# The last eleven expert tiles' results added to their tokens by TensorE through weighted one-hots, 48 tiles scattered as before

## The reference, cut to what matters

```python
x = x + 0.5 * ffn(layernorm(x))
x = x + attn(layernorm(x))        # silu gates, a causal filter, projections
x = x + 0.5 * ffn(layernorm(x))   # the same weights
# ffn: E = 12 experts, K = 3 per token, D = 128, H = 512
gate_logits = x @ Wg
topw, sel = top_k(gate_logits, K);  topw = softmax(topw)
h = gelu(x @ Wup[e] + bup[e]);      y = h @ Wdown[e] + bdown[e]
out[token] = sum over its 3 experts of topw * y
```

## Time and profile before

| | us |
|---|---|
| median of 3 runs | 648.72 |
| lowest, highest | 647.03, 653.67 |
| the profiled execution, its own time | 651.71 |
| its span, first to last instruction | 650.0 |

### The profile page before, as it was taken

The page is one execution under the profiler, slowest core; times in us unless marked ns, Lnnn a source line. Parts: engine busy times, 40 slices in busy tenths (PEclk is TensorE's granted clock), DMA queues, the critical chain, the costliest instruction groups (busy, mean ns, idle before and its releaser), DMA issues.

```text
span 650.0 us, 18112 instructions
## 1 busy us (share of the span) xinstructions
PE 567.4 (87%) x4607; PEld 530.7 (82%) x4607; DVE 350.8 (54%) x1644; ACT 415.1 (64%) x1265; POOL 418.6 (64%) x432
## 2 busy tenths in 40 slices
PE   4569999998988999999989799999988989999514
PEld 4448999998987888889989698878988989999501
DVE  7882365462115688887417578888541613232216
ACT  2235676685666789777658588886755846666223
POOL 1137777777767773077776777017777777777773
PEclk9768999999999999999989899999999989999857
DMA  9745767789796775365678777536569788776145
GB/s 236 220 142 140 211 201 195 214 202 265 201 271 201 231 198 177 98 186 155 221 205 245 220 239 203 155 101 183 179 182 262 193 253 262 221 216 196 46 163 184
DMA packets 121797, 127.89 MB, mean 197 GB/s; under 512 B 17129, under 2 KB 84512, under 8 KB 121700
## 3 DMA queue, kind: packets, MB, share of 16 engines
q1 hardware_dynamic: 107508, 100.05, 52.7%
q0 software_dynamic: 12992, 26.11, 14.4%
q10 hardware_dynamic: 1200, 0.59, 0.3%
HBM read 96.62 MB, written 30.79 MB: 196 GB/s over the span
## 4 chain that ended last, share of the span: by engine, by line
PE 42%; issue 16%; POOL 16%; DVE 11%; DMA 8%; SPq 4%; ACT 2%; POOLq 1%; ACTq 0%; DVEq 0%
PE ps L808 16%; PE ps L819 16%; POOL xs L619 7%; POOL YG L632 5%; POOL xl L606 2%; PE ps L690 2%; PE ps L778 2%; DMA YG<-ys,SY 2%; DMA ys<-Ys 2%; DVE X L1071 2%; SPq L474 1%; DMA xs<-XN,SX 1%; DVE YG L1425 1%; DMA WU<-in_L_ffn_Wup_dram 1%; SPq L490 1%
## 5 line engine op out<-in xcount | busy, mean ns | idle before, releaser
L969 ACT ACTIVATE hT<-ps,BU 128x128 f32<-128x128 f32 x944 | 269.6, 370 | 116.2 <-PE ps L808 114.1
L808 PE MATMUL ps<-xT,WU 128*128 128x128 f32 x1888 | 255.9, 279 | 13.4 <-DMA WU<-in_L_ffn_Wup_dram 8.5
L819 PE MATMUL ps<-WD,hT 128*128 x1888 | 253.1, 278 | 9.0 <-DVE Ys L1486 8.1
L808 PEld LDWEIGHTS ps<-xT,WU 128*128 128x128 f32 x1888 | 234.5, 194 | 24.2 <-issue 14.6
L819 PEld LDWEIGHTS ps<-WD,hT 128*128 128x128 f32 x1888 | 232.9, 194 | 10.2 <-issue 10.1
L619 POOL DMA_INDIRECT xs<-XN,SX x144 | 145.2, 1008 | 97.7 <-ACT XN L891 54.3
L1486 DVE TENSOR_TENSOR Ys<-ps,BD 128x128 f32<-128x128 f32 x236 | 67.7, 289 | 218.0 <-PE ps L819 213.8
L632 POOL DMA_INDIRECT YG<-ys,SY x144 | 149.6, 1039 | 52.1 <-issue 41.3
L606 POOL DMA_INDIRECT xl<-xn,SG x59 | 60.1, 1019 | 30.5 <-issue 17.1
L641 POOL DMA_INDIRECT yk<-Ys,row x59 | 59.0, 1000 | 18.0 <-issue 16.5
L946 ACT ACTIVATE xT<-ps 128x512 f32<-128x512 f32 (+1 forms) x56 | 33.3, 595 | 5.4 <-PE ps L778 2.0
(11 more groups left out here) (246 smaller groups left out, 526.3 us busy)
## 6 DMA issues: line engine op xcount, KB each, us to landing
WU<-in_L_ffn_Wup_dram SPq DMA_DIRECT2D x236, 256.0 KB
ys<-Ys SPq DMA_DIRECT2D x42, 256.0 KB, 2.4
xl<-xs SPq DMA_DIRECT2D x118, 66.0 KB, 2.4
xl<-xs SPq DMA_DIRECT2D x59, 64.0 KB, 1.9
WD<-in_L_ffn_Wdown_dram SPq DMA_DIRECT2D x12, 256.0 KB, 5.3
WD<-yk SPq DMA_DIRECT2D x4, 768.0 KB, 7.2
xs<-XN,SX POOLq DMA_INDIRECT x144
YG<-ys,SY POOLq DMA_INDIRECT x144, 3.2
```

What stands on the lines that cost most here:

```text
L808: x = e.matmul(HB[i % 2][:, c * P:(c + 1) * P], WU[i % NW][:, c * P:(c + 1) * P], xT[m % 2][:, j * P:(j + 1) * P], start=True, stop=True)
L819: x = e.matmul(YB[i % 2][:, 0:D], hT[i % 3][:, c * P:(c + 1) * P], WDf[:, bass.ds(r + c * P, P)], start=(c == 0), stop=(c == C - 1))
L969: x = e.activation(hT[i % 3][:, c * P:(c + 1) * P], HB[i % 2][:, c * P:(c + 1) * P], ACT.Gelu, bias=BU[:, bass.ds(b + c, 1)])
```

## The change

Phase 3 scatters only its first 4 x GO = 48 tiles. The results of the last NO = 11 tiles (48 to 58) never go to memory: for each, VectorE builds in `hots(x)` four tiles 128 x 512 (one for each quarter) that hold a row's weight where the column is that row's token, and TensorE multiplies them with `Ys` in `spread(x)`: 4 quarters x 4 blocks = 16 products 128x128x128 in float32, accumulated in `psum[4]` to `psum[7]`. To have the weight, the three top logits travel with the row (`DX[1]` = 135), ScalarE takes their exponential (step "OA", slots 45, 49, 51) and VectorE forms the weight (`weigh`, step "OV", slots 46, 50, 52). `hots(x)` stands in VectorE's slot 50 + x of the phase and `spread(x)` in TensorE's slot 51 + x, both at most 58. `last(q)` adds `psum[4 + q]` at its end and for that waits until all eleven spreads are done (`s_hd`); the identity products of quarters 0 and 2 add on top of the bank. Since `yk` gets no rows from eleven tiles, it is filled with zeros first: twelve stores of 256 KB by SyncE in slots 12 to 34 of phase 0. `YL`'s quarters 0 and 1 now lie over `XN` and are loaded before the last `down`; 2 and 3 stay over `WD`. `FETCHED` and `FINAL_AT` change, `xT` has three buffers.

```diff
-DX = (D, D + 4)
+DX = (D, D + 7)
...
-FETCHED = tuple(min(K * NT, 6 + (13 * k) // 25) for k in range(NTL))
-FINAL_AT = tuple(next((k + 8 for k in range(NTL - 8) if FETCHED[k] >= K * (t + 1)), NTL) for t in range(NT))
+GO = NG - 3
+NO = NTL - 4 * GO
+FETCHED = tuple(min(K * NT, 6 + (3 * k) // 5) for k in range(4 * GO))
+FINAL_AT = tuple(next((k + 12 + k // 15 for k in range(42) if FETCHED[k] >= K * (t + 1)), NTL) for t in range(NT))
+HOTS = [("A", "OA", 45, 0), ("V", "OV", 46, 0), ("A", "OA", 49, 1), ("V", "OV", 50, 1), ("A", "OA", 51, 2),
+        ("V", "OV", 52, 2)]
+HOTS += [("V", "H", min(4 * GO + x + 2, NTL - 1), x) for x in range(NO)]
+HOTS += [("P", "H", min(4 * GO + x + 3, NTL - 1), x) for x in range(NO)]
...
-        xT = [sb(f"xT{i}", [P, 512]) for i in range(2)]
+        xT = [sb(f"xT{i}", [P, 512]) for i in range(3)]
...
+        YL = [XN[h][:, :, :].rearrange("p t d -> p (t d)")[:, 0:4 * K * D].rearrange("p (t k d) -> p t k d", k=K, d=D)
+              for h in range(NH)] + [YLW[:, 0:4], YLW[:, 4:8]]
+        HOT = [sT, tg, ag]
...
+            def zero_yk(x):
+                if x == 0:
+                    e.wait_ge(s_iota, 2)
+                e.dma_start(yk.rearrange("(p t k) d -> p t k d", t=NT, k=K)[:, 4 * (x // K):4 * (x // K) + 4, x % K, :],
+                            ag[NQ - 1][:].rearrange("p (t d) -> p t d", d=D)).then_inc(s_zk, 16)
...
+                if n == 0 and k % 2 == 0 and 12 <= k < 12 + 2 * NQ * K:
+                    zero_yk((k - 12) // 2)
...
-            e.wait_ge(s_dn, NI)
-            for m in range(4 * NG - NYS, 4 * NG):
+            for m in range(3 * NG + GO - NYS, 3 * NG + GO):
                 e.wait_ge(*stored(m))
             for q in range(NQ):
+                if q == 2:
+                    e.wait_ge(s_dn, NI)
...
-            for x in range(NTL):
+            e.wait_ge(s_zk, 16 * NQ * K)
+            for x in range(4 * GO):
                 while got < FETCHED[x]:
                     gather_y(2, got // K, got % K)
                     got += 1
...
+            def spread(x):
+                i = NI - NO + x
+                m, j = 3 * NG + TILES[i][2] // 4, TILES[i][2] % 4
+                if x == 0:
+                    for b in range(NQ):
+                        e.wait_ge(*drained(LAST[b]))
+                e.wait_ge(s_ho, x + 1)
+                e.wait_ge(s_Y, i + 1)
+                for q in range(NQ):
+                    for t in range(4):
+                        z = e.matmul(psum[4 + q][:, t * P:(t + 1) * P], HOT[x % 3][q][:, t * P:(t + 1) * P],
+                                     Ys[m % NYS][:, j, :], start=(x == 0 and t == 0), stop=True, skip_group_check=True)
+                z.then_inc(s_hd, 1)
...
+                if kind == "OA":
+                    w = size(GO + q)
+                    e.wait_ge(s_ol, q + 1)
+                    e.activation(dl[:, 4 * q:4 * q + w, :], dl[:, 4 * q:4 * q + w, :], ACT.Exp).then_inc(s_oe, 1)
+                    e.activation(go[:, q:q + 1], one[:, 0:1], ACT.Gelu)
...
+            def weigh(x):
+                a, b = 4 * x, 4 * x + size(GO + x)
+                e.wait_ge(s_oe, x + 1)
+                dv.on(e.tensor_scalar(em[:, a:b, :], dl[:, a:b, 1:K], 1.0, None, ALU.subtract))
...
+            def hots(x):
+                if x >= 3:
+                    e.wait_ge(s_hd, x - 2)
+                e.wait_ge(s_dv, dv.n)
+                for q in range(NQ):
+                    i = e.tensor_scalar(HOT[x % 3][q][:], io5[:], tb[:, x, q:q + 1], wr[:, x:x + 1], ALU.is_equal, ALU.mult)
+                i.then_inc(s_ho, 1)
...
             def last(q):
...
+                e.wait_ge(s_hd, NO)
+                e.wait_ge(s_dv, dv.n)
+                x4 = X[:, 4 * g:4 * g + 4, :].rearrange("p t d -> p (t d)")
+                e.tensor_tensor(x4, x4, psum[4 + q][:], ALU.add).then_inc(s_fin, 1)
```

More of the change, by code:

```diff
@@ L138, in schedule @@
             put("V", NTL * 3 + FINAL_AT[t], f"F{t % 4}", 0, t // 4, 1)
+    for engines, kind, at, x in HOTS:
+        put(engines, NTL * 3 + at, kind, 1, x, 2)
     return slots
@@ L162, in next_group @@
         return NG * n
+    if n == 3 and k >= 4 * GO:
+        return {4 * GO: NG * n + NG - 2, 4 * GO + 2: NG * n + NG - 1}.get(k)
     if k and k % 4 == 0 and k // 4 + 1 < NG:
@@ L201, in ring @@
         for step in SLOTS["P"][i]:
-            take(step, RING[step[0]])
+            if step[0] != "H":
+                take(step, RING[step[0]])
     return used, last
@@ L255, in macaron_kernel @@
         toki, ytki = sb("toki", [P, NT], I32), sb("ytki", [P, NT], I32)
+        io5, qoff, tb = sb("io5", [P, 512]), sb("qoff", [P, NQ]), sb("tb", [P, NO, NQ])
+        dl, em, eqo = sb("dl", [P, NO, K]), sb("em", [P, NO, 2]), sb("eqo", [P, NO, 2])
+        wr, sl, rl = (sb(n, [P, NO]) for n in ("wr", "sl", "rl"))
         iopi, iop = sb("iopi", [P, P], I32), sb("iop", [P, P], F16)
@@ L576, in _ @@
             e.memset(ones[:], 1.0).then_inc(s_lt, 1)
+            e.iota(ag[2][:].bitcast(I32).rearrange("p (j r) -> p j r", r=P), [[K, 4], [K * NT, P]], base=0,
+                   channel_multiplier=0)
+            e.memset(ag[NQ - 1][:], 0.0).then_inc(s_iota, 1)
             e.wait_ge(s_iota, 1)
@@ L694, in side @@
                 kind, h, q, p = step
+                if kind == "H":
+                    spread(q)
+                    return
                 r, c = 4 * (2 * p + h) + q + 1, 4 * h + q + 1
@@ L1082, in side @@
                 kind, h, q, p = step
+                if kind in ("OV", "H"):
+                    weigh(q) if kind == "OV" else hots(q)
+                    return
                 r, c = 4 * (2 * p + h) + q + 1, 4 * h + q + 1
@@ L1472, in turn_x @@
[L1472 to L1476, removed]
+                    if g < GO:
+                        dv.on(e.scalar_tensor_tensor(dk[:, 0:k], eq[:, 0:k, 1], 2.0, eq[:, 0:k, 0], ALU.mult, ALU.add))
+                        e.wait_ge(s_dv, dv.n)
+                        if g >= NROW:
+                            e.wait_ge(*stored(m - NROW))
+                        e.tensor_tensor(row[g % NROW][:, 0:k], dk[:, 0:k], xl[m % NXL][:, 0:k, DX[1] - 1], ALU.add
+                                        ).then_inc(s_row, 1)
+                    else:
+                        at = 4 * (g - GO)
+                        lg = xl[m % NXL][:, 0:k, D + K:D + 2 * K]
+                        dv.on(e.tensor_tensor(
+                            tb[:, at:at + k, :], xl[m % NXL][:, 0:k, DX[1] - 1:DX[1]].to_broadcast([P, k, NQ]),
+                            qoff[:, :].rearrange("p (o q) -> p o q", o=1).to_broadcast([P, k, NQ]), ALU.subtract))
+                        e.tensor_tensor(dl[:, at:at + k, :], lg, lg[:, :, 0:1].to_broadcast([P, k, K]), ALU.subtract
+                                        ).then_inc(s_ol, 1)
@@ L1506, in _ @@
             e.tensor_copy(ioc[:], ioci[:])
+            e.tensor_scalar(qoff[:], ioci[:, 0:NQ], 4.0 * K / P, None, ALU.mult)
             e.tensor_copy(iop[:], iopi[:])
```

81 lines of the change are left out of this document (47 added, 34 removed).

## The result

| | before | after |
|---|---|---|
| median, us | 649.12 (4 runs) | 666.28 (4 runs) |
| ratio to before, 95% interval | | 1.023 (1.018 to 1.029) |
| profiled execution, own time / span | 651.71 / 650.0 | 668.08 / 666.3 |

The account below looks back on a forecast made before the run. TensorE is full to 610 us, GpSimd to 641. 39.3 + 3.0 + 0.9 put TensorE's end at 653.2; 9.9 + 5.3 + 1.0 give span 669.4, 19.4 over before: median 668 us, range 656 to 678.

Parts of the forecast that it names:

- What bounds: Phase 3's tail: TensorE full up to 610 us, then free; GpSimd, behind with scatters and gathers, full up to 641.
- The spreads, 39.3 us: TensorE, slots 51 to 58 and behind the last `down`: eleven spreads of 3.57 us, 39.3 us added in line.
- The wait before the first spread, 3.0 us: TensorE at slot 51 waits 3.0 us (2.0 to 3.7) for VectorE's weights and first one-hots.
- Clock: Rival: the wait at slot 51 lowers the clock, each spread 3.6 us more, two give 675; 0.16 with zeros, above 674.
- the stall that the prediction held against it: Against the clock rival: the clock stayed at 0.98 over 520 to 600 us with a 2 to 3 us stall.
- Exponential in slot 45, 0.9 us: ScalarE's first exponential with its table loads delays the gelu that `up(48)` waits for; TensorE loses 0.9 us.
- Zeros and wider rows, +1.0: Phase 0's twelve zero stores and half 1's 2.3% wider rows: 1.0 us together, range 0 to 7.5.
- VectorE's end, 9.9 us: Behind the last spread, VectorE's bank adds, blocks 12 to 15 and `last(3)` stand in line: 9.9 us, to 663.1.
- The store, 5.3 us: The last store, behind VectorE's last block, takes 5.3 us and ends at 668.4.
- Sum: Whole kernel: all terms give a span of 669.4 us, 19.4 over 650.0; median 668.
- GpSimd still sets the end: Rival at the kernel's end: spreads fit beside the rest, span 635.6, time 634, if a spread is under 0.6 us; 0.07.

Follow-up runs that it names:

- e1: Changed kernel with each spread issuing 8 of its 16 products (the half kernel): 651.06 us, ratio to before 0.997.
- e2: Changed kernel with each spread issuing 4 of its 16 products (the quarter kernel): 646.62 us, ratio to before 0.991.
- h1: Kernel of g2 (three tiles by one-hots) once more, on a chip where the kernel before takes 651.53 us: 645.24 us, ratio to before 0.995.
- e3: Changed kernel with the one-hots of the first three tiles built in VectorE's slots 47 to 49 instead of 50 to 52: 664.22 us, ratio to before 1.019.
- g2: Changed kernel with three tiles by one-hots, scatters ahead of more gathers, VectorE's end reordered; all kernels 1.5 times as long: 966.70 us, ratio to before 1.011.

## Why the prediction was right, by its own steps

- **What bounds.** Two limits that pass each other, GpSimd's backlog and TensorE's full slots. e1, e2 and h1 bear it out. Missing from it was a third: VectorE's row behind `down(58)`. And GpSimd's line was not followed to its end: behind the last gather comes the DRAIN.
- **The spreads, 39.3 us.** Ten of eleven took 3.57 us and stood in the chain; `down(58)` ends at 639.60, as forecast (near 639). Taking half of their products away removed the loss. Right.
- **The wait before the first spread, 3.0 us.** 2.43. Its term for the one-hots, 2.4 us for four, was too high: the first four took 2.04 us, the later sets 1.9 to 2.2, one instruction 540 ns. Here the rule of the Trainium skill ("VectorE: DVE Perf Modes", the perf-mode tier table), some 1.8 us by estimate, was nearer than my value between the rows.
- **Clock.** The rival came true in a small way: first spread 5.44 us at a granted clock of 0.68, 1.87 us that the sum lacked. Its condition, the wait, is not enough: the quarter kernel has the same wait and no loss. Nor was the stall that the prediction held against it harmless: behind 2.23 us at 525 us in the kernel before, eight instructions took 2.08 us instead of 0.89.
- **Exponential in slot 45, 0.9 us.** 1.02. The trip took 3.0 us from load to gelu:

```profile
583.62 1.28 ACT L926 ACT_TABLE_LOAD   x1
584.92 0.21 ACT L926 ACTIVATE dl<-dl 128x12 f32<-128x12 f32 x1
585.15 1.28 ACT L927 ACT_TABLE_LOAD   x1
586.44 0.20 ACT L927 ACTIVATE go<-one 128x1 f32<-128x1 f32 x1
587.82 1.13 PE L865 MATMUL ps<-xT,WU 128*128 128x128 f32 x8 [1.02 <-ACT hT L1034]
```

  The drain that the Trainium skill ("ScalarE: Activation LUTs", What ACT_TABLE_LOAD costs) counts beside a load shows here no more than before: the next instruction starts 0.01 to 0.02 us behind each load.
- **Zeros and wider rows, +1.0.** Not seen: phase 3 starts 2.1 us earlier than in the profile of before. There is only one such profile, so what the change has to do with it stays open. Within phase 3 TensorE then loses 1.3 us more than before up to the last spread, beyond the terms above; in 484 to 520 us the granted clock is 0.91 instead of 1.00. The last spread ends at 653.91, forecast 653.2. That this is so close is in part luck: clock and phase 3 cost 3.2 us more than forecast, the early start and the shorter wait gave 2.6 back.
- **VectorE's end, 9.9 us.** 9.5 (653.93 to 663.40).
- **The store, 5.3 us.** 2.9 in the changed kernel. This is the term that was mis-sized most, 2.4 us, and the row was misread: the 5.3 us behind VectorE in the kernel before were not the store. The store was over 1.6 us behind VectorE, at 646.3; the last 3.4 us were GpSimd's DRAIN. Where GpSimd is done earlier, the end lies 2.9 us behind VectorE in the changed kernel, 3.0 in e3, 2.3 in e1 and e2; in h1, where it is last again, 5.4.
- **Sum.** 19.4 us forecast, 16.3 between the spans. Less than forecast: behind VectorE 2.4, start of phase 3 2.1, zeros 1.0, wait 0.6, VectorE's end 0.4. More: clock 1.9, phase 3 on TensorE 1.3, exponential 0.1.
- **The rival "GpSimd still sets the end"** was priced wrongly. For spreads of 0.89 us, as in e2, its formula (610.04 + 3.9 + 11s + 15.2) gives 638.9 and GpSimd's line 635.6; the span was 643.6, because VectorE, not GpSimd, is next in line (GpSimd's DRAIN is over at 633.0).

## What to carry to other kernels

An idle engine is only idle where it is idle: seven of the eleven spreads went into slots that TensorE already filled, and all eleven lay in front of a wait that held up VectorE's whole end. Fit the moved work to the valley (here 20 us of TensorE: three tiles at 3.57 us fit, eleven don't; four and five were not tried) and price each tile on both engines, 1.3 us off the one, 3.6 us onto the other. And when pricing the removal of a bottleneck, list every in-order row that starts at the same point, not only the two engines that trade work. And before the time behind the last compute instruction is called a store, look at when the store landed and which queue is done last.

## What the runs showed of the hardware that was not expected

- GpSimd's queue is not done when its last gather has landed. In the kernel before the gather starts at 639.93 and has landed at 643.38, but the DRAIN lasts until 649.7. In the six undisturbed profiles the DRAIN ends 9.7 to 10.1 us behind the start of the last gather. It set the end of the program where GpSimd was last (the kernel before and h1), and cost nothing elsewhere. What it waits for is not in the traces.
- Waits of 2.4 us of TensorE at the same place were followed by a granted clock of 0.68 over 5.4 us (2.43, the changed kernel), 0.51 over 3.4 us (2.37, half) and 1.00 (2.40, a quarter); one of 1.13 us (e3) by 1.00. What decides stays open. The kernel before has both too: eight instructions behind a 2.23 us wait at 525 us took 2.08 us, those behind a 2.77 us wait at 499 us went on at about the usual pace:

```profile
499.26 0.94 PE L808 MATMUL ps<-xT,WU 128*128 128x128 f32 x6 [2.77 <-DMA WU<-in_L_ffn_Wup_dram]
525.36 2.08 PE L808 MATMUL ps<-xT,WU 128*128 128x128 f32 x8 [2.23 <-DMA WU<-in_L_ffn_Wup_dram]
```

- On two of the four chips of the experiments all kernels took about 1.5 times as long. The instructions have their usual durations (GpSimd's DMAs 1.0 us, the gelu 373 ns); what grows is idle time that no instruction of the program ends. The waits of g2 over its whole span:

```profile
DVE Ys L1593 <- remote: 303.6, 35, 36.1
ACT hT L1034 <- remote: 230.0, 39, 36.0
...
PEld ps L865 <- issue: 150.8, 103, 11.0
```

  "remote" is a releaser that is not in the trace. The cause stays open. It changed a verdict: the same kernel with three tiles is 0.5% faster than before without it (h1) and 1.1% slower with it (g2). With slow tiles GpSimd has no backlog to take away, and the spreads themselves are stretched.
